# Issuing the transfers that clear the routed rows behind a pass's second weights instead of behind its packing

## What is computed

```python
x = _layernorm(x + _L0_attn_ref(x, wq_down, wq_up, wq_rope, q_norm_w, wkv_down, kv_norm_w, wkv_up, wk_rope, wo))
x = _layernorm(x + _L0_xattn_ref(x, ctx_512, Wq, Wkv_expand, Wout))
x = _layernorm(x + _L0_ffn_ref(x, gate_w, gate_b, ew1, eb1, ew2, eb2, sw1, sb1, sw2, sb2))

# in _L0_attn_ref
q_c = _rms_norm(x @ wq_down.T, q_norm_w)
q_nope = (q_c @ wq_up.T).reshape(bs, seq_len, NH, D_NOPE)
q_pe = _apply_rope((q_c @ wq_rope.T).reshape(bs, seq_len, NH, D_ROPE), cos, sin)
kv_c = _rms_norm(x @ wkv_down.T, kv_norm_w)
kv_up = (kv_c @ wkv_up.T).reshape(bs, seq_len, NH, D_NOPE + D_V)
...
probs = jax.nn.softmax(scores, axis=-1)
out = jnp.einsum('bhqk,bkhd->bqhd', probs, v).reshape(bs, seq_len, NH * D_V)
return out @ wo.T

# in _L0_ffn_ref: topv, topi = top_k(softmax(xf @ gate_w + gate_b), 2)
h = gelu(einsum('nd,edh->neh', xf, ew1) + eb1)
routed = einsum('ned,ne->nd', einsum('neh,ehd->ned', h, ew2) + eb2, combine)
```

## Time and profile before

| | before |
|---|---|
| time, median of 3 | 851.8 us (851.23 to 852.64) |
| time of the profiled execution | 852.53 us |
| its span | 850.7 us |
| mean granted TensorE clock | 0.991 of full speed |
| PE busy | 820.5 us, 96% |
| DVE, ACT, POOL busy | 531.7, 456.6 and 241.2 us |

### The profile page before, as it was taken

How to read it: one execution, slowest core, us unless ns; L and a number is a source line. 1 busy time by engine, 2 the same in 40 slices (tenths; PEclk the granted TensorE clock), 3 DMA queues, 4 the chain that set the end, 5 groups by cost and what they waited for, 6 DMA issues and landing times.

```text
span 850.7 us, 13303 instructions
## 1 busy us (share of the span) xinstructions
PE 820.5 (96%) x4270; PEld 700.7 (82%) x4270; DVE 531.7 (63%) x994; ACT 456.6 (54%) x1189; POOL 241.2 (28%) x284
## 2 busy tenths in 40 slices
PE   7999999799899999999997999999999999999997
PEld 5887888688688888888885888888888888889885
DVE  4757756654564677687787657265655655646466
ACT  6427535443554466977786616153755737547050
POOL 0142311032132132655654003502232322321420
PEclk9999999899989999999999999999999999999999
DMA  9113214230611346333112204534554655644422
GB/s 340 67 44 112 68 40 129 106 105 21 213 62 43 86 135 201 92 68 74 37 21 69 75 25 133 214 109 139 190 195 134 233 168 171 201 147 137 134 76 87
DMA packets 41598, 99.99 MB, mean 118 GB/s; under 512 B 15889, under 2 KB 23953, under 8 KB 39921
## 3 DMA queue, kind: packets, MB, share of 16 engines
q1 hardware_dynamic: 30496, 61.62, 22.9%
q0 software_dynamic: 11056, 37.79, 13.6%
HBM read 71.59 MB, written 20.97 MB: 109 GB/s over the span
## 4 chain that ended last, share of the span: by engine, by line
PE 78%; SPq 7%; DVE 4%; DMA 4%; ACT 3%; issue 3%; POOL 1%; DVEq 0%; ACTq 0%; POOLq 0%
PE ps L1549 63%; SPq L555 4%; DMA stage<-in_wa 3%; PE ps L1896 2%; PE ps L1570 2%; PE ps L1609 2%; PE ps L1712 2%; PE ps L1886 1%; SPq L575 1%; PE ps L1780 1%; ACT Pt L886 1%; POOL ro_lo L700 1%; DMA kb<-kx 1%; PE ps L1898 1%; PE ps L1720 1%
## 5 line engine op out<-in xcount | busy, mean ns | idle before, releaser
L641 POOL TENSOR_TENSOR Pt<-Pt,rowinv 112x448 f32<-112x448 f32 x64 | 59.6, 935 | 183.4 <-DVE rowinv L1153 183.2
L886 ACT ACTIVATE Pt<-ps,negmax 112x112 f32<-112x112 f32 x256 | 87.2, 358 | 26.9 <-DVE negmax L1146 26.4
L1549 PE MATMUL ps<-x2T_hi,ws_hi 128*128 128x448 f32 x256 | 95.2, 372 | 1.7 <-DVE x2T_lo L1090 1.7
L1549 PE MATMUL ps<-x2T_hi,ws_lo 128*128 128x448 f32 x256 | 93.6, 366 | 0.0
L1549 PE MATMUL ps<-x2T_lo,ws_hi 128*128 128x448 f32 x256 | 93.6, 366 | 0.0
L1549 PE MATMUL ps<-w_hi,h_hi 128*128 128x512 f32 x224 | 89.9, 401 | 0.0
L1549 PE MATMUL ps<-w_hi,h_lo 128*128 128x512 f32 x224 | 88.4, 395 | 0.0
L1549 PE MATMUL ps<-w_lo,h_hi 128*128 128x512 f32 x224 | 88.4, 395 | 0.0
L1017 ACT ACTIVATE hf<-ps,b 128x448 f32<-128x448 f32 x64 | 40.6, 634 | 88.0 <-PE ps L1549 68.7
L1090 DVE TENSOR_TENSOR h_lo<-hf,h_hi 128x448 fp32r<-128x448 f32 x64 | 39.9, 624 | 45.5 <-ACT h_hi L1018 45.0
L1435 DVE TENSOR_TENSOR acc<-ps,acc 128x512 f32<-128x512 f32 x56 | 38.5, 689 | 45.4 <-PE ps L1549 37.7
(11 more groups left out here) (289 smaller groups left out, 2215.0 us busy)
## 6 DMA issues: line engine op xcount, KB each, us to landing
stage<-in_wf SPq DMA_DIRECT2D x30, 513.0 KB
rows_in<-in_zeros SPq DMA_DIRECT2D x30, 256.0 KB, 3.8
xs<-rows_in POOLq DMA_DIRECT2D x29, 256.0 KB, 4.2
rows_out<-yb POOLq DMA_DIRECT2D x29, 256.0 KB
stage<-in_wa SPq DMA_DIRECT2D x4, 1408.0 KB, 8.1
stage<-in_wb SPq DMA_DIRECT2D x4, 1280.0 KB, 5.5
qr<-ro_hi SPq DMA_DIRECT2D x64, 56.0 KB, 1.9
qr<-ro_lo SPq DMA_DIRECT2D x64, 56.0 KB, 1.9
```

The costliest lines, as they stand in the source:

```text
L641: nc.gpsimd.tensor_tensor(p, p, rowinv[0:S, b % 2, :].unsqueeze(2).broadcast_to([S, GH, S]), ALU.mult).then_inc(norm_done, 1)
L886: last = nc.scalar.activation(Pt[0:S, b % 2, h * S:(h + 1) * S], ps[0:S, b % 2, h * S:(h + 1) * S], ACT.Exp, bias=negmax[0:S, b % 2, h:h + 1],
L1549: ins = mm(dst, w, x, start=start and i == 0, stop=stop and i == len(ops) - 1, skip_group_check=not (start and stop))
```

## The change

The loop over the ten clearing transfers moves up within the body of the loop of line 567: from behind `pack(g, 1)`, where the next thing SP does is to load the next group's first weights, to behind `load_b(g)` and ahead of `pack(g, 0)`. Nothing is added or removed, and no wait changes.

```diff
                 sp.wait_ge(bw_lo, g * len(B_PIECES))
                 sp.dma_start(stage[:, 0:A_SIZE], d["wa"][g, :, :]).then_inc(st_ld, 16)
                 load_b(g)
+                for i in range(NZERO):
+                    sp.dma_start(rows_in[i, g - 1, :, :], d["zeros"]).then_inc(zero_st, 16)
                 pack(g, 0)
                 pack(g, 1)
-                for i in range(NZERO):
-                    sp.dma_start(rows_in[i, g - 1, :, :], d["zeros"]).then_inc(zero_st, 16)
```

## The result

The changed kernel takes 839.32 us (median of 4 runs, 838.27 to 840.60) against 851.98 us for the kernel before (median of 4 runs, 851.23 to 852.64). The ratio is 0.9847, 95% interval 0.9832 to 0.9863: faster by 11.7 to 14.3 us, where 12.5 were forecast. Run again beside other kernels later, it took 839.87 us at a ratio of 0.9837 (0.9815 to 0.9859). Its profiled execution took 838.27 us, with a span of 836.3 us.

The account below looks back on a forecast made before the run. PE was taken as the bound, stopped twice by late first weights behind the clearing; 9.5 us of waits and 3.0 us of clock gave 12.5 us off the 851.8 us median: 839.3 us, range 838.0 to 843.0.

Parts of the forecast that it names:

- What bounded the kernel: PE, busy 96% of the span, stopped twice ahead of `O` 0 for late first weights, 9.5 us together, plus slower clock.
- Step 1: Load of the next first weights on SP: issued 4.3 and 4.2 us sooner, 0.3 us after DVE's last read of `stage`.
- Step 2: That load, with the DMA engines to itself, lands in 6.2 us instead of 7.82 or 8.32, 5.9 us sooner.
- Step 3: Ahead of `O` 0: weights ready before PE needs them, with 0.4 us over on DVE and 1.4 us on the load.
- Step 4: Both PE stops and the slow matmuls behind them go: 4.54 + 1.67 + 4.99 + 1.35 = 12.55 us.
- Steps 5 and 6: Clearing behind `load_b`: SP's 8.7 us idle wait hides 6.94 us of issues; sharing DMA with second weights and packing costs nothing.
- A: Rival: PE's idle time comes back, the clock's part doesn't; gain 9.5 us, time 842.3 us; chance 0.08.
- B: Rival: load of first weights still late; small waits 840 to 841 us, late end 845 to 848 us, chance 0.05.
- C: Rival: no effect on this path, because SP's wait for `stage` (line 569) opens too late; 851.8 us; chance 0.03.
- D: Rival: slower, packing delayed so ACT waits at `ro_hi` and PE behind it in three passes; 853.5 us; chance 0.03.

Follow-up runs that it names:

- the experiment without it: Against the kernel before, the ten clearing transfers moved out of attention into the cross-attention loop, behind the load of the next weights: 839.03 us, ratio 0.9841.

## Why the prediction was right

**What bounded the kernel**: right. Both stops ahead of `O` 0 are gone, the dips of the clock with them, and nothing after the attention stage changed: from the load of group 3's second weights to the clearing of `kb` before the keys are 72.4 us in both profiles.

**Step 1**, the issue of the load: right. It was to come 0.3 us after DVE's last read and not when SP is free; DVE's read, from 142.74 for 1.22 us, ends at 143.96 and the issue comes at 144.13. SP waits 2.8 us there, off the path.

**Step 2**, the landing: right in size, 6.1 and 5.9 us in the two passes where 6.2 was taken. But the split behind it doesn't hold. The prediction said that the clearing costs the path twice, 4.3 us of SP's time and 1.7 to 2.2 us of shared DMA engines, as if one could be had without the other. Issues alone (ten small transfers) cost 3.13 and 2.43 us of waiting. Bytes cost more than the split gives once the load is issued on time: with five transfers ahead it took 8.75 and 8.35 us, 2.2 to 2.7 us more than 6.1, which is more for half the bytes than the split has for all of them. So taking away the issue time alone would not have given back 4.3 us. With all the bytes in one transfer the load took 13.24 us and the kernel a ratio of 1.0019, where the split priced 840 to 841 us; how much of that is bytes, and how much that they moved only ten packets at a time, isn't separated. What the runs support is that the two costs overlap instead of adding up: the load can land no sooner than about 6 us after its issue, and no sooner than 3.7 to 5.4 us after the last packet ahead of it. No single rate gives that last packet, as the run with half the clearing shows. The change takes away both at once, so the error cost the forecast nothing.

**Step 3**, the margin: right, on DVE and at 0.34 us.

**Step 4**, the sum: right within its error, with one term too small. Measured from one load of the second weights to the next, a pass falls from 75.38 us (95.12 to 170.50) and 75.47 to 68.57 us: 6.81 and 6.90 us, 13.7 together, not 12.5. The baseline was not clean. The first load, of group 1, had landed only just in time, and the matmuls behind `O` 0 took 3.89 us where undisturbed ones take 3.47. In the kernel with half the clearing, at full clock, the stretch behind its stop is 3.88 us as well (155.25 to 159.13). So a late load costs, beside the wait and the clock, about 0.4 us in the matmuls right behind it, and 0.6 us over the whole pass. That PE there runs into work that ACT and DVE have begun late is my reading. Against the clean 3.47 the stretches behind the stops are 2.09 and 1.77 us too long, where the sum had 1.67 and 1.35; with the waits that is 13.4 us of the 13.7.

The pair of profiles differs by 14.4 us in span: 13.7 in these two passes, 0.7 ahead of them, where SP starts the first packing 0.4 us sooner (65.78 for 66.16) and gets it done in 10.0 instead of 10.7 us. That lead has no part in the gain of the passes: in the second profile of the changed kernel the second weights of group 1 are issued at 95.81, later than before, and its passes are as short. Medians and ratio give 12.7 and 13.0 us with an interval of 11.7 to 14.3, which holds both the forecast and the 13.7.

**Steps 5 and 6**, the new place: right. It costs nothing, by the experiment without it; the second weights aren't delayed. The first packing transfer does report late, 3.4 us after its issue at 103.45 where 1.9 us is the median: at 106.85, behind the clearing's last packet at 106.48. The prediction allowed for this, up to 109.8, and nobody waits for it. The slack is as large as I had read, 11 us to ACT's rounding (12.5 us of lateness give a wait of 1.04), and about 2 us more before PE notices (ACT waits 8.75 where PE waits 6.69). Where I was wrong is what is behind it: I expected the packing's own readers on PE to be the next to wait, and it is the queries that ACT makes after its rounding.

**The rivals.** A, the idle time back without the clock's part, can be set aside in the profile: 0.999 of full clock. B, a load still late, is what half the clearing brings about, with waits of 1.92 and 1.45 us. C and D didn't come about.

## What to carry to other kernels

A bulk transfer with a distant deadline belongs behind the loads that an engine is about to need, not ahead of one. Here, on the one queue that SP issues to, 2.62 MB behind a load cost it nothing, and the same transfers ahead of it cost 13 us over two passes, by their bytes and by SP's time for their issues. To price such a place look at both, what stands ahead in bytes and when the load can be issued, and take the later instead of adding them up.

Merging the issues into one transfer did not help here. Before it is tried elsewhere, count how many packets the merged transfer has in flight: this one had ten where the separate ones had up to 16.

When a pass is used as the undisturbed reference for another, check that its own load came early enough and not just in time, or the gain comes out too small.

## What was not expected of the hardware

**The clock after short stops.** A late transfer makes thirteen stops of PE of over 1 us in these profiles. The four of 1.03, 1.45, 1.58 and 1.92 us left the granted clock at 1.00 in the 5.5 us behind them. The nine of 2.43 to 7.46 us all had it between 0.50 and 0.70 there. The figure doesn't follow the length: 0.69 after 2.43 us, 0.50 after 3.13, 0.60 after 4.54 and 5.58, 0.50 after 5.91. So in these executions a late load that stopped PE for less than 2 us cost no clock. Each kernel has one profiled execution, and the four of the ten small transfers, from 844.32 to 849.69 us, show that the clock's part differs between them. The Trainium skill (TensorE: Matmul & The Clock Gate, "What's actually happening") has a gate that watches activity on a schedule of its own, and the spread of these figures agrees with it.

**One large copy had fewer packets in flight than ten small ones.** The 2.62 MB in one transfer moved in 40 packets of 64 KB, ten at a time, and took 11.0 us from first packet to last; in ten transfers of 256 KB they moved in 160 packets of 16 KB, up to 16 at a time, and took 9.4 us although SP needed 6.9 us to issue them. Behind the one the load took 13.24 and 13.59 us, and the kernel was 0.1 to 0.3% slower than with the ten.
